# Weight loads ahead of the turning transfers in the gate stage, and row normalisation on ScalarE in the projections

## The reference

```
x = x + window_attention(ln(x))     # 16 heads, window of 128 to each side, output projection
x = x + moe(ln(x))                  # 8 experts, top 2, and one shared expert
x = x + block_attention(ln(x))      # 16 heads, blocks of 64
x = x + ternary_linear(ln(x))       # weights quantised to -1, 0, 1
```

```
logits = xf @ gate_w.T;  top-2 of 8, softmax over the two -> comb
out = sum over e of comb[:, e] * (silu(xf @ wg[e].T) * (xf @ wu[e].T)) @ w_down[e].T
shared = silu(xf @ sg_gate.T) * (xf @ sg_up.T) @ sg_down.T
```

## Time and profile before

| | |
|---|---|
| median of three runs | 3210.08 us |
| profiled execution | 3220.43 us, span 3218.7 us |
| mean granted clock of TensorE | 0.832 |
| PE busy | 2391.7 us (74%) |
| DVE busy | 2043.7 us (63%) |
| ACT busy | 1565.5 us (49%) |
| POOL busy | 984.4 us (31%) |

### The profile page before, as it was taken

One profiled execution on the slowest core, in us unless ns is written; L12 is line 12 of the kernel. 1 busy time (PEld: TensorE's weight loads), 2 busy tenths in 40 slices (PEclk: granted clock), 3 DMA queues, 4 the chain that ended last, 5 costly groups with the idle time before them and its releaser, 6 DMA issues. The chain is left out here.

```text
span 3218.7 us, 81517 instructions
## 1 busy us (share of the span) xinstructions
PE 2391.7 (74%) x25933; PEld 1381.7 (43%) x25933; DVE 2043.7 (63%) x5809; ACT 1565.5 (49%) x3598; POOL 984.4 (31%) x1271
## 2 busy tenths in 40 slices
PE   7917888888856645668799996783588888888336
PEld 4602222222215534556688885441133333333225
DVE  7827777777715544445444443991789888887278
ACT  5605666666650023334244442551278777778202
POOL 3503433434434014556466664341000000000005
PEclk9957877878876667778899998896699999999658
DMA  6521222222201114444555344563022222221123
GB/s 205 201 87 32 63 64 68 64 62 69 68 29 55 42 49 118 115 122 138 118 130 145 90 90 101 189 230 113 21 68 65 62 65 62 63 67 46 52 72 104
DMA packets 361817, 290.14 MB, mean 90 GB/s; under 512 B 226304, under 2 KB 294656, under 8 KB 361408
## 3 DMA queue, kind: packets, MB, share of 16 engines
q1 hardware_dynamic: 348448, 249.32, 27.2%
q0 software_dynamic: 12960, 35.54, 3.4%
HBM read 133.46 MB, written 123.62 MB: 80 GB/s over the span
## 5 line engine op out<-in xcount | busy, mean ns | idle before, releaser
L766 ACT ACTIVATE a_pr<-a_pst 128x384 f32<-128x384 f32 (+3 forms) x2176 | 935.9, 483 | 398.7 <-PE a_pst L790 360.7
L714 DVE TENSOR_REDUCE a_mx<-a_psc 128x1 f32<-128x384 f32 (+2 forms) x1152 | 592.2, 567 | 140.1 <-PE a_psc L790 130.3
L709 DVE CUSTOM_DVE_ANT_0 a_cut<-a_psc,row_mask 128x384 bf16<-128x384 f32 (+1 forms) x1024 | 499.7, 522 | 209.1 <-PE a_psc L790 174.6
L857 PE MATMUL a_po<-a_pr,a_ve 128*17 128x128 f32 (+3 forms) x10496 | 622.8, 328 | 1.6 <-ACT a_pr L766 1.0
L790 PE MATMUL a_psc<-a_ke,a_qe 52*128 52x128 f16 (+5 forms) x3072 | 411.8, 312 | 249.5 <-DMA a_ke<-mrow 114.5
L790 PE MATMUL a_pst<-a_qe,a_ke 53*128 53x128 f16 (+5 forms) x3072 | 399.4, 303 | 104.4 <-ACT a_pr L766 44.3
L688 POOL TENSOR_SCALAR_AFFINE_SELECT a_pr<-a_pr 128x512 f32<-128x512 f32 x448 | 275.0, 634 | 496.2 <-ACT a_pr L766 496.2
L1796 POOL TENSOR_TENSOR x_res<-x_res,t_bias 128x256 f32 (+1 forms) x64 | 44.5, 726 | 967.4 <-DVE t_xn L185 967.4
L790 PEld LDWEIGHTS a_pst<-a_qe,a_ke 53*128 53x128 f16 (+1 forms) x3072 | 122.6, 95 | 468.3 <-ACT a_pr L766 234.3
L790 PEld LDWEIGHTS a_psc<-a_ke,a_qe 52*128 52x128 f16 (+1 forms) x3072 | 130.0, 97 | 407.1 <-issue 160.2
L857 PEld LDWEIGHTS a_po<-a_pr,a_ve 128*17 128x17 f32 x10496 | 198.3, 98 | 239.0 <-issue 154.8
(11 more groups left out here) (217 smaller groups left out, 4324.0 us busy)
## 6 DMA issues: line engine op xcount, KB each, us to landing
a_qe<-qx SPq DMA_DIRECT2D x384, 64.0 KB, 2.6
a_ke<-kx SPq DMA_DIRECT2D x384, 64.0 KB, 2.6
vx<-p_vst SPq DMA_DIRECT2D x32, 544.0 KB, 3.1
a_ve<-vx SPq DMA_DIRECT2D x64, 272.0 KB, 3.2
ox<-a_ost SPq DMA_DIRECT2D x256, 68.0 KB
c_ot<-ox SPq DMA_DIRECT2D x32, 544.0 KB
qx<-p_stg SPq DMA_DIRECT2D x64, 256.0 KB, 3.3
kx<-p_stg SPq DMA_DIRECT2D x64, 256.0 KB, 3.1
```

The source lines that it names most:

```text
L709: dve.tensor_tensor_reduce(out=cut[:, n % 4, 0:width], in0=psc[n % RING][:, 0:width], in1=row_mask[:, at:at + width], scale=1.0, scalar=-3 ...
L714: dve.tensor_reduce(out.unsqueeze(1), psc[n % RING][:, 0:width], AXX, ALU.max)\
L766: act.activation(pr[s % SLOTS][:, h // 2, h % 2, 0:width], pst[k % RING][:, 0:width], ACT.Exp, scale=scale).then_inc(p_ready, 1)
L857: last = pe.matmul(po[h][32 * a:32 * a + VW, tok % CH:tok % CH + w], ve[g][:, t, a * VW:(a + 1) * VW], pr[s % SLOTS][:, a // 2, a % 2, col ...
```

## The change

In the gate stage, SP issues load(2) ahead of turn(0), and in each step the loads of the step ahead of turn(s+2). In the projection stages, the subtraction of the mean and the multiplication by 1/std move from DVE to ACT: DVE computes 1/std and shift = -mean/std for the chunk (`invert`), ACT computes x times 1/std plus shift in four activations (`norm`), which in turn c stand ahead of the third of the four q/k groups. norm(0) and norm(1) stand around the weight casts, ahead of high(0); invert(1) moves up beside invert(0).

```
-            def norm(c):
+            def invert(c):
                 k = c % 2
                 dve.wait_ge(rooted, ONE + c + 1)
+                if c >= 2:
+                    dve.wait_ge(normed, ONE + TC * (c - 1))
                 dve.reciprocal(rstd[:, k, :], std[:, k, :]).then_inc(inverted, 1)
                 dve.wait_ge(inverted, ONE + c + 1)
                 dve.wait_ge(gathered, ONE + TC * (c + 1))
-                if c >= 2:
-                    dve.wait_ge(turned, ONE + EC * (c - 1))
-                for t in range(TC):
-                    dve.tensor_scalar(xn[:, k, t, :], x_res[:, c * TC + t, :], mv[:, k, t, 0:1], rstd[:, k, t:t + 1],
-                                      ALU.subtract, ALU.mult).then_inc(normed, 1)
+                dve.scalar_tensor_tensor(out=shift[:, k, :], in0=mv[:, k, :, 0], scalar=-1.0, in1=rstd[:, k, :],
+                                         op0=ALU.mult, op1=ALU.mult).then_inc(shifted, 1)
...
             statistics(0)
             statistics(1)
-            norm(0)
+            invert(0)
+            invert(1)
...
             low(0)
-            norm(1)
             statistics(2)
...
                 if c + 2 < NC:
-                    norm(c + 2)
+                    invert(c + 2)
...
+            def norm(c):
+                k = c % 2
+                if c >= 2:
+                    act.wait_ge(turned, ONE + EC * (c - 1))
+                act.wait_ge(shifted, ONE + c + 1)
+                for t in range(TC):
+                    act.activation(xn[:, k, t, :], x_res[:, c * TC + t, :], ACT.Identity, bias=shift[:, k, t:t + 1],
+                                   scale=rstd[:, k, t:t + 1]).then_inc(normed, 1)
...
                 for m in range(4):
+                    if m == 2 and c + 2 < NC:
+                        norm(c + 2)
                     act.wait_ge(qk_ready, ONE + 4 * c + m + 1)
...
             root(1)
+            norm(0)
             act.wait_ge(s_w, ONE + 64)
             for j in range(3):
                 act.activation(wh[:, j], w32[:, j], ACT.Copy, scale=WS).then_inc(s_wh, 1)
+            norm(1)
             high(0)
...
             for n in range(2):
                 load(n)
+            load(2)
             turn(0)
-            load(2)
             turn(1)
             for s in range(NC + 2):
+                for n in weight_parts(s):
+                    load(n)
                 if s + 2 < NC:
                     turn(s + 2)
-                for n in weight_parts(s):
-                    load(n)
```

More of the change, by code:

```diff
@@ L235, in stage_project @@
         st, mv = sb("st", [P, 2, TC, 6], F32), sb("mv", [P, 2, TC, 2], F32)
-        std, rstd = sb("std", [P, 2, TC], F32), sb("rstd", [P, 2, TC], F32)
+        std, rstd, shift = (sb(n, [P, 2, TC], F32) for n in ("std", "rstd", "shift"))
         xn = sb("xn", [P, 2, TC, D], F32)
@@ L248, in stage_project @@
         merged, seen, gathered = sem("merged"), sem("seen"), sem("gathered")
-        rooted, inverted, normed = sem("rooted"), sem("inverted"), sem("normed")
+        rooted, inverted, shifted, normed = sem("rooted"), sem("inverted"), sem("shifted"), sem("normed")
         turned, hi_done, lo_done = sem("turned"), sem("hi_done"), sem("lo_done")
```

## The result

On the chip of the first comparison the changed kernel took 3123.97 us (median of four runs, 3113.10 to 3132.45), the kernel before 3214.06 (a fourth run, 3219.72, beside the three shown above): ratio 0.9726, interval 0.9674 to 0.9778. It is faster, by 90 us of the 122 forecast, and lies 2 us outside the range. The profiled executions, 3220.4 and 3132.45 us, differ by 88.0: the gate stage gave 92.5 (forecast 99.0), the second projection 2.2 (forecast 24.0), the first nothing, and the gate stage began 6.5 us later, after a long stretch of code that is the same in both.

The account below looks back on a forecast made before the run. Late expert-weight loads held gate steps; PE bounded the first projection, DVE the second. Terms -101.7 + 2.7 - 25.4 + 1.4 + 0.5 = -122.5 took 3220.4 to 3097.9 us, less 10 for the median: 3088, range 3056 to 3122.

Parts of the forecast that it names:

- Gate stage, steady part: Twelve gate steps with weight conversion: loads arrive in time, twelve ACT waits go, step 23.7 to 15.2 us, -101.7 us.
- That 0.3: Gate step: 0.3 us added for POOL's subtractions running beside DVE's weight conversions, giving 15.2 us.
- Gate start: Start of the gate stage: load(2) ahead of turn(0) delays the first top2, +2.7 us.
- First projection: First projection stage: PE still bounds it at 8.67 us a chunk, ACT's added work fits; +0.5 us.
- Second projection: Second projection stage: chunk falls from 11.56 to 9.6 us, -25.4 us, with +1.4 us at its start.
- The sum, 19.2 us, spans two chunks: 9.6 each: Second projection: the new path through PE, DVE and ACT sets the chunk at 9.6 us, PE idle for 0.9.
- term of 5.86 us to the root: Second projection path: time from the second vst copy to ACT's root, put at 5.86 us.
- 8.0 us a chunk of the forecast: Second projection: DVE's need after losing four tiles and gaining one tiny multiply, 11.6 to 8.0 us a chunk.
- Rival B: Second projection: the path through ACT costs as much as DVE's work did, only the gate gains; 3111 us, chance 0.12.
- D's sum: Gate stage: loads stay late because their buffers free late, only the projections gain; 3188 us, chance 0.03.
- a chunk of 10.3 us: Second projection by the skill's rule: DVE loses only 1.4 us a chunk, gain about 16 us in place of 25.
- C: Gate stage: a new wait from crowded transfers or POOL not keeping up, step 18.5 us; 3127 us, chance 0.09.

Follow-up runs that it names:

- e7: Changed kernel, but DVE does each gate step's second weight conversion in the next step, ahead of row_lo; ratio to the kernel before 0.9651.
- e6: Changed kernel with POOL's gate-stage subtraction cut to 8 of 256 columns; ratio to the kernel before 0.9648.
- e4: Kernel before with POOL's subtraction in both projections cut to 8 of 512 columns; ratio to the kernel before 0.9902.
- e3: Changed kernel with POOL's subtraction in both projections cut to 8 of 512 columns; ratio to the kernel before 0.9636.
- e12: Changed kernel with ACT's root(c+2) moved behind the first two projection evictions, right before norm(c+2); ratio to the kernel before 0.9740.
- e10: Changed kernel with DVE's statistics(c+3) ahead of values(c) and experts' results loaded two chunks earlier in the projections; ratio to the kernel before 0.9675.

## Why the prediction was right and where it failed

**Gate stage, steady part: right in mechanism, 6.0 us short.** The loads come in time, twelve waits went, and the clock was 0.99 over the twelve steps. The step was put at 13.65 and the growth of the leg, 1.26, with 0.3 added for POOL's subtractions beside DVE's conversions. That 0.3 is the term mis-sized. The leg took 6.31 us in place of 5.48, so the collision cost 0.83, and 13.65 + 1.26 + 0.83 = 15.74 against the 15.70 measured. In the step from which the leg was read a collision was there too, but POOL paid for it. These are rows of the kernel before, in the leg that starts at 1237.20, POOL's and then DVE's:

```profile
1238.16 2.04 POOL L1250 TENSOR_TENSOR g_hl<-g_hid,g_hh 128x256 f16<-128x256 f32 x2 [5.65 <-ACT g_hh L1290]
```

```profile
1238.72 0.95 DVE L1318 SCALAR_TENSOR_TENSOR dl<-g_w,dh 128x768 f16<-128x768 f32 x1
1240.02 1.00 DVE L1318 SCALAR_TENSOR_TENSOR ul<-g_w,uh 128x768 f16<-128x768 f32 x1 [0.35 <-ACT uh L1267]
```

ACT had been blocked, so POOL had sat idle for 5.65 us and began 0.96 us into the leg. Its second subtraction met the first conversion, which kept its 0.95 us, and the pair took 2.04 us where e7 has 1.31; it was over at 1240.20, soon after the second conversion began. In the changed kernel nothing holds the step back, and POOL is still at its scatters at that point:

```profile
1297.12 1.34 POOL L1254 DMA_INDIRECT xs<-g_xrow,g_slot  x1 [0.30 <-issue]
```

So its pair starts 3.32 us into the leg, at 1298.48, in the middle of the second conversion, and now DVE pays too: 1.36 and 0.88 us for its last two rows, with 2.19 for POOL's pair. With e6 the leg is back at 5.52.

**Gate start: right.** DVE's first use of the gate logits moved by the 2.7 us forecast, from 14.98 to 17.68 us after the stage's first normalisation; row_hi(2) moved by 3.0. PE's first product came 17 us after the stage's start, as forecast.

**First projection: right.** 8.67 us and no cost; ACT's four tiles took 602 ns in the median.

**Second projection: the step that failed.** It said: "The sum, 19.2 us, spans two chunks: 9.6 each". The path is the right one, PE, values, merges, root, evictions, normalisation, transposes, and with POOL light it measured 19.4. But its term of 5.86 us to the root was read where the merges stood alone; POOL's subtractions fell on the tensor_scalars then, which is why those took 1240 ns, and 407 in e4. With the tensor_scalars gone, DVE does the merges at that moment, and it is they who wait: 7.1 to 8.0 us in place of 5.25 from their start to the root, and 22.6 us for two chunks in the mean. For the same reason DVE's own need was not the 8.0 us a chunk of the forecast but 9.9. The gain was 3.1 us in the loop in place of 25.4, less 2.3 at the start (1.4 forecast) and plus 1.4 at the end.

Rival B had nearly the right time for the stage, some 11.5 us a chunk, for a wrong reason: it had the path through ACT cost what DVE's work had. What passes on the cost is POOL. That its 3111 lies near the measured 3124 is no support for it: it is 13 us too low, and the gate stage, which fell short by 6.5 us, and the 6.5 ahead of it make up as much. (D's sum, 3210 - 23.5, is 3187 and not 3188; nothing rests on it.)

The rule of the Trainium skill, "ScalarE: Activation LUTs", section Rules for kernel authors, that multiplies belong on VectorE was weighed with a chunk of 10.3 us. With POOL light, in e4 against e3, it is right: 407 ns a tile on DVE, 602 on ACT, and the move to ACT costs 0.8 us a chunk. What made the move look good was a row that measured contention.

**Ahead of the gate stage: +6.5 us, inside the spread of that stretch.** From the first projection's last copy of v to the gate stage's first normalisation the code is the same in all kernels. The stretch took 1009.80 us in the kernel before (165.50 to 1175.30) and 1016.60 in the changed kernel (165.20 to 1181.80), at granted clocks of 0.74 and 0.75; the first projection ended 0.3 us sooner. Over the profiled executions of thirteen kernels here the stretch ranged from 1008.0 to 1027.5 us. Both ends belong to kernels with the changed projection, e12 and e10, and the kernel before was near the low end. No range of mine had a term for this, and what makes it vary is open.

**The range.** A miss of 6 us in the gate stage, 22 in the projection and 6.5 of spread all fell on one side. B and C had each been given their own place; both happening in part was not priced.

## What to carry to other kernels

A row that takes three times its own minimum may measure a collision and not the instruction: before you move it away, ask what it collides with, and which instruction will stand there next. Ask also who paid: in the gate stage the same two kinds of instruction collided before and after, first at POOL's cost alone and then, when POOL came later, at DVE's as well. Move the neighbour's work in the sum as well: when a wait goes, every engine that was held by it shifts, and durations taken from the old overlap no longer hold. Here moving DVE's work to ACT gave 3.1 us of 25.4, because POOL's subtractions made DVE slow wherever they met it; the levers that worked were POOL's own work (e3, e6) and DVE's order against POOL (e7, e10).

## What the runs showed of the hardware

- Ten DVE merges of 128x256 took 4.05 us alone and 9.17 beside POOL subtractions, ten bn_stats 3.37 and 3.36, ten instructions with one of two operands in PSUM 6.07 and 6.07. POOL suffers too: six subtractions 7.49 us beside bn_stats, 11.11 beside the 128x768 conversions.
- A POOL subtraction cut to 8 columns took 0.19 to 0.22 us in the gate stage where DVE read no two operands from SBUF beside it. When it began just after row_lo it took 1.20: at 1292.15 in e6, with row_lo from 1292.06 to 1293.31, it ended at 1293.36. So a small POOL instruction can wait for all of a long DVE one.
- The same projection code ran its 13 chunks in 147.1 us at granted clock 0.95 (three executions), in 144.0 at 0.97 and in 142.9 at 0.99. PE waited ahead of the transposes in all of them (23.4 us in ten waits at 0.95, 24.2 in twelve at 0.99). Where the clock fell inside a chunk, PE's part of it took 10.6 us in place of 8.9; what picks the clock is open.
